# Cross-attention of a decoder layer: inverse sums spread by VectorE shuffles, logits in eight products, low halves on GpSimd in every step

## What is computed

```
scores = clip(q k^T / sqrt(32), -50, 50), masked; probs = softmax(scores)     # 16 heads of 32
probs  = probs / (sum(probs) + 1e-8);  ctx = probs v
delta  = layernorm(rs * (ctx Wo^T + bo)) * gamma + beta
x      = x + delta
logits = layernorm(x) @ gate_weight^T;  scores = softmax(logits)              # 64 experts
```

## Time and profile before

| | us |
|---|---|
| runs | 1539.0, 1537.34, 1533.39 (median 1537.34) |
| the profiled execution's own time | 1540.01 |
| its span, first to last instruction | 1538.3 |
| PE busy in the span | 1464.2 (95%) |
| DVE busy | 1115.0 (72%) |
| ACT busy | 941.6 (61%) |
| POOL busy | 688.1 (45%) |
| mean granted clock of PE | 0.984 |

### The profile page before, as it was taken

How to read it: one execution, slowest core, us unless ns; L and a number is a source line. 1 busy time by engine, 2 the same in 40 slices (tenths; PEclk the granted TensorE clock), 3 DMA queues, 4 the chain that set the end, 5 groups by cost and what they waited for, 6 DMA issues and landing times.

```text
span 1538.3 us, 30281 instructions
## 1 busy us (share of the span) xinstructions
PE 1464.2 (95%) x10344; PEld 1216.4 (79%) x10344; DVE 1115.0 (72%) x1959; ACT 941.6 (61%) x1769; POOL 688.1 (45%) x830
## 2 busy tenths in 40 slices
PE   6999999899999979689999999999999999999988
PEld 4788887678888867578888898888888888876766
DVE  5677676636788788777777777777777777757756
ACT  4556566644656556677777777778777777741110
POOL 2122124342232146355556555555555555347763
PEclk9999999999999999889999999999999999999999
DMA  6012122242121141299877788777887788567664
GB/s 212 1 63 83 37 75 70 73 124 70 56 90 43 43 125 49 88 330 342 283 269 268 264 295 275 271 265 268 298 271 269 268 272 299 193 216 246 191 185 151
DMA packets 116629, 280.25 MB, mean 182 GB/s; under 512 B 17984, under 2 KB 23104, under 8 KB 116544
## 3 DMA queue, kind: packets, MB, share of 16 engines
q1 hardware_dynamic: 98800, 228.25, 43.7%
q0 software_dynamic: 15360, 50.34, 10.7%
q10 hardware_dynamic: 2384, 0.53, 0.2%
HBM read 235.69 MB, written 43.38 MB: 181 GB/s over the span
## 4 chain that ended last, share of the span: by engine, by line
PE 50%; issue 3%; DVE 3%; DVEq 1%; ACT 0%; DMA 0%; SPq 0%
PE e_gu L2615 18%; PE e_gu L2618 9%; PE e_dn_rest L2644 6%; PE e_tr L49 3%; PE e_dn_main L41 3%; PE e_dn_main L43 3%; PE e_dn_main L42 3%; DVE h_acc L2909 1%; DVEq L2938 1%; PE h_dn L41 1%; PE h_dn L42 1%; PE h_dn L43 1%; PE h_gt L41 0%; PE h_gt L43 0%; PE h_gt L42 0%
## 5 line engine op out<-in xcount | busy, mean ns | idle before, releaser
L2377 POOL TENSOR_TENSOR e_hid<-e_h_raw,e_hid 128x256 fp32r<-128x256 f32 (+1 forms) x128 | 128.9, 1007 | 225.7 <-ACT e_hid L2443 225.7
L2615 PE MATMUL e_gu<-e_xT_hi_lo,e_wu 128*128 128x384 f32 (+1 forms) x768 | 223.9, 346 | 0.0
L2615 PE MATMUL e_gu<-e_xT_hi_lo,e_wg 128*128 128x384 f32 (+1 forms) x768 | 221.8, 343 | 0.4 <-issue 0.4
L2618 PE MATMUL e_gu<-e_xT_hi_lo,e_wu 128*128 128x192 f32 (+1 forms) x768 | 157.8, 260 | 0.0
L2385 POOL TENSOR_TENSOR e_wd<-e_raw_d,e_wd 96x512 fp32r<-96x512 f32 x64 | 132.6, 2071 | 55.5 <-ACT e_wd L2427 55.5
L2618 PE MATMUL e_gu<-e_xT_hi_lo,e_wg 128*128 128x192 f32 (+1 forms) x768 | 152.2, 253 | 0.0
L2519 DVE TENSOR_TENSOR e_total<-e_gu,e_low 128x384 f32<-128x384 f32 x192 | 106.1, 553 | 48.3 <-issue 38.9
L2508 DVE TENSOR_TENSOR e_wg<-e_raw_g,e_wg 128x1408 fp32r<-128x1408 f32 x64 | 104.1, 1627 | 45.8 <-ACT e_wg L2418 45.3
L2618 PEld LDWEIGHTS e_gu<-e_xT_hi_lo,e_wg 128*128 128x128 f32 (+1 forms) x768 | 135.2, 180 | 0.0
L2618 PEld LDWEIGHTS e_gu<-e_xT_hi_lo,e_wu 128*128 128x128 f32 (+1 forms) x768 | 134.8, 179 | 0.0
L2439 ACT ACTIVATE e_low<-e_gu 128x384 f32<-128x384 f32 x192 | 93.9, 489 | 59.9 <-issue 49.1
(11 more groups left out here) (427 smaller groups left out, 3941.2 us busy)
## 6 DMA issues: line engine op xcount, KB each, us to landing
e_raw_g<-in_L_ffn_Wg_dram SPq DMA_DIRECT2D x64, 704.0 KB
e_raw_u<-in_L_ffn_Wu_dram SPq DMA_DIRECT2D x64, 704.0 KB
e_raw_d<-in_L_ffn_Wd_dram SPq DMA_DIRECT2D x64, 512.0 KB
y_dram<-e_y_main SPq DMA_DIRECT2D x64, 256.0 KB
e_raw_d<-in_L_ffn_Wd_dram SPq DMA_DIRECT2D x64, 192.0 KB
y_dram<-e_y_rest SPq DMA_DIRECT2D x64, 128.0 KB
s_xr<-in_x_dram SPq DMA_DIRECT2D x16, 256.0 KB
x_dram<-s_x SPq DMA_DIRECT2D x16, 256.0 KB, 2.6
```

The costliest lines, as they stand in the source:

```text
L2377: pool.tensor_tensor(hid[b][1][:, part, :], h_raw[g.odd][b][:, part, 0:P], hid[b][0][:, part, :].bitcast(F32), ALU.subtract).then_inc(s_hl, 1)
L2615: pe.matmul(gu[(b + c) % 2][0:n, at, 0:2 * CAP], w[b][0][:, k, m:m + n], xT[:, :, k, toks], start=k == 0, stop=False)
L2618: ins = pe.matmul(gu[(b + c) % 2][0:n, at, 0:CAP], w[b][1][:, k, m:m + n], xT[:, 0, k, toks], start=False, stop=k == KC - 1)
```

## The change

- PE's `widen` and ACT's `rinv_out` go, with the constant `spread` and the use `("rb", t)` of bank `ex[1]`. DVE has `spread_rinv(t)` between `bounded(t+1, 0)` and `attn_out(t)`: four shuffles, each sends row c of every 32 rows of `rinv` to all 32 rows of a 128-column piece of `rb`. After the loop it stands in front of `delta(14)`.
- The gate's halves lie side by side (`gate_both`). `logits` has, for each of four k, one product of 128 columns (hi with both halves) and one of 64 (lo with the high half). The three terms are the same as before; they now lie in two 64-column halves of the bank.
- `route_max` sums the two halves from PSUM into `prob` (this releases the bank) and then takes the maximum from SBUF. `route_exp` works in place on `prob` and signals `s_le`, for which `rank_experts` waits.
- `attn_lo` and `final_lo` leave DVE. POOL makes all of them, from step 1 and step 2 on. ACT makes the raw copy in every `final_hi`, into a buffer of its own, and waits for the `final_lo` of the batch before.

```diff
@@ cross_uses
-        ex[1] += [("rb", t - 1)] if 1 <= t <= BATCH else []
@@ buffers
-        gate = [sb("gate_hi", [P, KC, E], F32R), sb("gate_lo", [P, KC, E], F32R)]
+        gate_both = sb("gate_hi_lo", [P, KC, 2, E], F32R)
+        gate = [gate_both[:, :, half, :] for half in range(2)]
-        spread = sb("spread", [P, KC, HPC, HD])
-        final_raw = kept["x"][3][:]
+        final_raw = sb("final_raw", [P, H])[:]
+        def logit_of(t):
+
+            g = group_of(t)
+            return prob[g % 2][:, t - CROSS_GROUPS[g][0], :]
@@ gpsimd
-                if t >= LAST:
+                if t >= 1:
                     attn_lo(t - 1)
...
-                if t >= LAST:
+                if t >= 2:
                     final_lo(t - 2)
@@ scalar
-            def rinv_out(t):
-                act.wait_ge(s_rb, t + 1)
...
-                act.activation(rb[:], ex[1][:], ACT.Copy).then_inc(s_er[1], 1)
@@ final_hi
-                if t < LAST - 2:
-                    act.activation(final_T(t)[0], ex[0][:].rearrange("p (k s) -> p k s", k=KC), ACT.Copy).then_inc(s_fh, 1)
-                else:
...
+                if t:
+                    act.wait_ge(s_fl, t)
+                act.activation(final_raw, ex[0][:], ACT.Copy)
+                act.activation(final_T(t)[0], ex[0][:].rearrange("p (k s) -> p k s", k=KC), ACT.Copy).then_inc(s_er[0], 1)
@@ route_exp
-                if g >= 2:
-                    act.wait_ge(s_choice, g - 1)
-                act.activation(prob[g % 2][:, t - CROSS_GROUPS[g][0], :], ex[0][:, 0:E], ACT.Exp, bias=lneg[:, t:t + 1],
-                               accum_out=lsum[:, t:t + 1]).then_inc(s_er[0], 1)
+                act.activation(logit_of(t), logit_of(t), ACT.Exp, bias=lneg[:, t:t + 1],
+                               accum_out=lsum[:, t:t + 1]).then_inc(s_le, 1)
@@ vector
+            def spread_rinv(t):
+
+                dve.wait_ge(s_er[1], exchanged(1, ("sum", t)))
+                if t:
+                    dve.wait_ge(s_er[0], exchanged(0, ("pv", t - 1)))
+                for c in range(KC):
+                    dve.stream_shuffle(rb[:, c * P:(c + 1) * P], rinv[:], [c] * HD).then_inc(s_rb, 1)
@@ attn_out
-                dve.wait_ge(s_er[1], exchanged(1, ("rb", t)))
+                dve.wait_ge(s_rb, KC * (t + 1))
@@ route_max
-                dve.tensor_reduce(lneg[:, t:t + 1], ex[0][:, 0:E], AX, ALU.max, negate=True).then_inc(s_lm, 1)
+                if group_of(t) >= 2:
+                    dve.wait_ge(s_choice, group_of(t) - 1)
+                dve.tensor_reduce(logit_of(t), ex[0][:, 0:2 * E].rearrange("p (h e) -> p e h", h=2), AX, ALU.add
+                                  ).then_inc(s_er[0], 1)
+                dve.wait_ge(s_er[0], exchanged(0, ("lg", t)))
+                dve.tensor_reduce(lneg[:, t:t + 1], logit_of(t), AX, ALU.max, negate=True).then_inc(s_lm, 1)
@@ vector loop
                 bounded(t, 0)
                 if t >= 1:
+                    spread_rinv(t - 1)
                     attn_out(t - 1)
                 bounded(t, 1)
...
-                if LAST > t >= 1:
-                    attn_lo(t - 1)
...
-                if LAST > t >= 2:
-                    final_lo(t - 2)
@@ tensor
-            def widen(t):
-                out = exchange(1, ("rb", t))
-                for c in range(KC):
-                    ins = pe.matmul(out[:, c * P:(c + 1) * P], spread[:, c, :, :].rearrange("p j d -> p (j d)"), rinv[:],
-                                    start=True, stop=True)
@@ logits
-                if t < LAST - 2:
-                    pe.wait_ge(s_er[0], exchanged(0, ("xf", t)))
-                else:
-                    pe.wait_ge(s_fl, t - LAST + 3)
+                pe.wait_ge(s_fl, t + 1)
                 for k in range(KC):
-                    ins = matmul3(pe, out, (hi[:, k, :], lo[:, k, :]), (gate[0][:, k, :], gate[1][:, k, :]),
-                                  k == 0, k == KC - 1)
+                    pe.matmul(out[:, 0:2 * E], hi[:, k, :], gate_both[:, k, :, :].rearrange("p h e -> p (h e)"),
+                              start=k == 0, stop=False)
+                    ins = pe.matmul(out[:, 0:E], lo[:, k, :], gate[0][:, k, :], start=False, stop=k == KC - 1)
```

More of the change, by code:

```diff
@@ L1129, in cross_phase @@
         s_aw = sem("attn_ready")
-        s_ft, s_fh, s_fl = sem("xfT_in_psum"), sem("xfT_hi_ready"), sem("xfT_lo_ready")
-        s_lg, s_lm = sem("logits_in_psum"), sem("logit_max_ready")
+        s_ft, s_fl = sem("xfT_in_psum"), sem("xfT_lo_ready")
+        s_lg, s_lm = sem("logit_halves_in_psum"), sem("logit_max_ready")
+        s_le = sem("logit_exp_ready")
         s_choice, s_pos, s_posr = sem("choice_ready"), sem("positions_in_psum"), sem("positions_read")
@@ L1339, in constants @@
                 lk(pool.memset(pick[:, 0, KC:HD], 1.0))
-                lk(pool.memset(spread[:], 0.0))
-                lk(pool.affine_select(out=spread[:], in_=spread[:], pattern=[[-1, KC], [-HD, HPC], [0, HD]],
-                                      compare_op=ALU.not_equal, fill=1.0, base=0, channel_multiplier=1))
                 pool.memset(mark[:], 0.0).then_inc(s_pick, 1)
@@ L1733, in rank_experts @@
                 grouped = pr.rearrange("p t (g n) -> p (t g) n", g=GROUPS)
-                dve.wait_ge(s_er[0], exchanged(0, ("lg", b - 1)))
+                dve.wait_ge(s_le, b)
                 link(dve.reciprocal(lsum[:, a:b], lsum[:, a:b]))
@@ L1888, in _ @@
             one, two, three = range(NG - 3, NG)
+            spread_rinv(BATCH - 1)
             delta(BATCH - 2)
@@ L2010, in logits @@
             def logits(t):
-                out = exchange(0, ("lg", t))[:, 0:E]
-                if t < LAST - 2:
-                    pe.wait_ge(s_er[0], exchanged(0, ("xf", t)))
-                else:
-                    pe.wait_ge(s_fl, t - LAST + 3)
+                out = exchange(0, ("lg", t))
+                pe.wait_ge(s_fl, t + 1)
                 hi, lo = final_T(t)
                 for k in range(KC):
-                    ins = matmul3(pe, out, (hi[:, k, :], lo[:, k, :]), (gate[0][:, k, :], gate[1][:, k, :]),
-                                  k == 0, k == KC - 1)
+                    pe.matmul(out[:, 0:2 * E], hi[:, k, :], gate_both[:, k, :, :].rearrange("p h e -> p (h e)"),
+                              start=k == 0, stop=False)
+                    ins = pe.matmul(out[:, 0:E], lo[:, k, :], gate[0][:, k, :], start=False, stop=k == KC - 1)
                 ins.then_inc(s_lg, 1)
@@ L2024, in shared_unit @@
                 if i == 0:
-                    pe.wait_ge(s_fl, QT * AHEAD + QT - LAST + 2)
+                    pe.wait_ge(s_fl, QT * (AHEAD + 1))
                 pe.wait_ge(s_flo, i + 1)
@@ L2033, in shared_unit @@
                     elif i == EARLY + 1:
-                        pe.wait_ge(s_er[1], exchanged(1, ("rb", BATCH - 1)))
+                        pe.wait_ge(s_er[1], exchanged(1, ("sum", BATCH - 1)))
                     elif i == EARLY + 2:
@@ L2128, in _ @@
             shared_unit(4)
-            widen(BATCH - 1)
             positions(BATCH, one)
```

22 lines of the change are left out of this document (2 added, 20 removed).

## The result

The changed kernel takes 1543.11 us (median of 7 runs, 1540.52 to 1544.53) and the kernel before 1536.39 us beside it (7 runs, 1533.13 to 1539.0). The ratio is 1.0045 with the 95% interval [1.0033, 1.0058]: slower by some 7 us, just inside the 0.5% that counts as no change. I had forecast 1534.7 us, a gain of 2.7. The result lies 0.1 us above the top of my range, and on the other side of the kernel before. The profiled execution took 1542.32 us, span 1540.6, mean clock 0.979 (before: 1540.01, 1538.3, 0.984).

What follows compares the result with a forecast made beforehand. TensorE, nearly matched by a chain through VectorE over step pairs, bounds steps 1 to 11; VectorE's small operations pace the late steps. Terms sum to 2.7 us saved off the 1537.34 us median: 1534.7 us, range 1525 to 1543.

Steps and rivals of the forecast that it cites:

- The bound of steps 1 to 11: Each odd-even step pair: VectorE's chain nearly matches TensorE's work; slack 0.46 us in steps 5 and 6, further gain becomes waiting.
- I had 1.5 to 2.5 for 6 and 10: Steps 6 and 10: TensorE idle in front of L2056 by 1.5 to 2.5 us, released by `bounded`.
- full gains in steps 1 to 4, 7 and 8: Savings of 2.0 us in steps 1 and 2, 1.8 in 3 and 4, about 1.5 in 7 and 8.
- I charge 0.3 us in the light steps: Final rows' low half on GpSimd: logits start later, 0.3 us charged in light steps, hidden behind the larger wait in pairs.
- the 14.5 I took off: TensorE's gain at most: widening 10.0 us in steps 1 to 11, logits 4.5 us in steps 2 to 11.
- my estimate of 0.4 us for one: VectorE shuffle of 128 elements by the skill's page: 400 ns, 1.6 us for four; the forecast used 1.2 us.
- Low halves and lock: Attention low half: no stall; GpSimd products hold VectorE operations, 0.5 us in each odd step from 5, bounds 0 and 2.2.
- steps 13 and 14 +1.5 and the tail +1.3: Steps 13 and 14 lose 1.5 us, as VectorE only gains work; step 15 and the tail lose 1.3 us.
- Locks and bubbles: Rival, pairs 3/4 to 11/12: locks lengthen chains 7.5 us, low clock after idle adds 3; 1545.2 us, chance 0.10.

Runs made afterwards that it cites:

- the kernel in which it went: Kernel after, with TensorE's positions moved behind the second projection unit in steps 2 to 10: 1544.26 us, ratio 1.0047 to the kernel before.
- three moves: Kernel before with shuffles and short logits in steps 1 to 11, positions later, final rows' low half before keep_slots, fresh rows' before that: 1534.54 us, ratio 0.9955.

## Why the prediction was wrong

*The bound of steps 1 to 11.* Right in kind: the chain through VectorE over a pair is nearly as long as TensorE's work, and TensorE's gain turns into a wait at the positions (1.98, 0.61 and 2.05 us in steps 6, 8 and 10; I had 1.5 to 2.5 for 6 and 10). Wrong in extent. I counted full gains in steps 1 to 4, 7 and 8, where no positions stand in the way or the chain has room: -5.3 together, measured -1.9. The steps that failed are "I charge 0.3 us in the light steps" for the final rows' low half, and that I charged nothing for a unit's bank. The 0.3 us is what the low halves alone cost (0.26 at the logits of step 4), but a TensorE that is ahead by the widening waits 0.7 to 1.1 us at the same place. In all, the waits are 3.7 us for the final rows' low half and 4.2 (1.6 before) for the bank. The profile of before shows that row for the bank, and I read it as small when it was next in line: the shuffles-and-logits kernel has the same 4.2 us without any low half on GpSimd.

*Widening and logits.* Sized well. Eight products take 0.88 us from 443.18 to 444.06. One of 128 columns and one of 64 together take 0.22, what two of 64 took before. TensorE's busy time fell by 12.6 us with both parts, of the 14.5 I took off. In steps 9 and 10 a term was missing: the low clock behind the wait at the positions, 1.7 us by the kernel in which it went.

*Shuffles.* Their price was right: 1.0 us for four against 1.2. The Trainium skill, "VectorE: DVE Perf Modes", the perf-mode tier table, led to my estimate of 0.4 us for one; the row has 0.298, and 0.21 from one start to the next, so the measurement decides.

*Low halves and lock.* Attention rows: no stall and no cost, as forecast. The lock was 0.75 to 0.8 us in each of the five odd steps from 3 on, where I charged 0.5 from step 5 on. The rule of the Trainium skill, "SBUF — State Buffer", Who interferes with whom, agrees with the trace: shuffles (0.298), the sum from PSUM (0.274) and the attention product (0.69) were never held.

*Late steps, where the kernel lost most.* I gave steps 13 and 14 +1.5 and the tail +1.3, and took widenings saved on TensorE off the delays. Measured are +3.4 and +3.9, and +1.5 for 11 and 12. The widening is not in the round that sets these steps, so nothing was to be saved; the shuffles are, in full, each time round. And longer idle time brought low clock over the output projection and the products behind it, which I had priced at nothing in the forecast though I had the row (2.10 for 1.18 us in the earlier trace rows). The low clock was in the rival "Locks and bubbles", whose 1545.2 us were 2 us from the result. That nearness is luck: the rival needed 2.5 us more in every pair, from the lock, and had nothing for the shuffles in the late round. What came is 0.7 and 2.0 us in two pairs and 8.8 us behind them.

## What to carry to other kernels

Work that leaves a busy engine is worth its time only where that engine is the bound; where it sits in the engine's idle time it is worth nothing, and moving it into the round of small operations that does set the pace costs it once per round. Here four shuffles cost 1.02 us in every late round, while the widening that they replaced had cost none. So price such a change stage by stage, follow the round once around in the trace, and keep the old form in the stages where the other engine sets the pace. When a gain disappears, look for the next wait in the queue before blaming the first: here easing one brought 1.6 us and three moves brought 3.6 us of steps 1 to 11 (194.1 to 190.5). And measure the whole: with steps 1 to 11 6.4 us shorter, the stage was 1.5 us shorter.

## What was not expected of the hardware

The granted clock repeats: low stretches stood behind the same idle gaps in every profile of the same program, to 0.7 us, and the same code behind other early steps took up to 3.5 us more in steps 12 to 14 at a lower clock. In the logits a product of 128 columns with one of 64 takes as long as two of 64 (0.22 us). Shuffles of 128x128 overlap: 0.298 us each, one every 0.21 us, and setting the pattern shows as 0.014 us.
